# Four graph layers on one core: rows that empty edge slots read, and the order of the last twelve halves of two attentions

## The reference, cut to what matters

```python
x = _layernorm(x + _L0_gnn_ref(...))   # two GCN convolutions
x = _layernorm(x + _L1_gnn_ref(...))   # GAT attention, 8 heads
x = _layernorm(x + _L2_gnn_ref(...))   # HGT attention, 8 heads, 8 node and 8 edge types
x = _layernorm(x + _L3_gnn_ref(...))   # edge pass, summed by src
# the pattern, as in _gat_forward:
e = e_u[src] + e_v[dst]; m = segment_max(e, dst); ex = exp(e - m[dst])
agg = segment_sum(table[src] * (ex / segment_sum(ex, dst)[dst]), dst)
```

## Time and profile before

| | us |
|---|---|
| runs | 7548.39, 7556.19 (median), 7559.97 |
| profiled execution | 7554.35, its span 7552.5 |
| POOL busy | 4883.0 (65% of the span) |
| PE busy, PE weight loads | 4910.9, 3728.8 |
| DVE busy | 4682.7 (62%) |
| ACT busy | 3188.4 (42%) |
| gathers of c1, c2, gat (L757) | x2496, 978 ns each |
| gathers of hgt (L757), edge pass (L2750) | x832 at 982 ns, x832 at 956 ns |

### The profile page before, as it was taken

The page is one execution under the profiler, slowest core; times in us unless marked ns, Lnnn a source line. Parts: engine busy times, 40 slices in busy tenths (PEclk is TensorE's granted clock), DMA queues, the critical chain, the costliest instruction groups (busy, mean ns, idle before and its releaser), DMA issues. The chain is left out here.

```text
span 7552.5 us, 95692 instructions
## 1 busy us (share of the span) xinstructions
PE 4910.9 (65%) x26906; PEld 3728.8 (49%) x26906; DVE 4682.7 (62%) x12437; ACT 3188.4 (42%) x7393; POOL 4883.0 (65%) x4968
## 2 busy tenths in 40 slices
PE   8999801666676777774365655856656666777774
PEld 6777601444444455553254544435555543555553
DVE  8999801555554577775456666645666566566666
ACT  0222200444443444442244444746665642555553
POOL 0677775777776777774777773047777700777774
PEclk9776655888887888886566666967887787899997
DMA  1333201222223222223666665567777822766665
GB/s 29 79 82 79 58 2 28 52 55 55 56 55 48 53 56 55 56 55 56 168 180 183 183 183 118 195 196 230 231 230 224 221 69 82 217 209 210 209 208 146
DMA packets 817681, 925.24 MB, mean 123 GB/s; under 512 B 120147, under 2 KB 656219, under 8 KB 816923
## 3 DMA queue, kind: packets, MB, share of 16 engines
q0 software_dynamic: 198144, 441.54, 23.4%
q1 hardware_dynamic: 395118, 365.43, 16.2%
q10 hardware_dynamic: 223916, 112.15, 5.1%
HBM read 724.85 MB, written 193.87 MB: 122 GB/s over the span
## 5 line engine op out<-in xcount | busy, mean ns | idle before, releaser
L757 POOL DMA_INDIRECT arena<-t,d_src x2496 | 2441.0, 978 | 902.6 <-issue 759.2
L796 PE MATMUL ps<-arena 128*128 128x128 f32 (+2 forms) x8320 | 1779.4, 374 | 755.9 <-DMA arena<-t,d_src 623.5
L796 PEld LDWEIGHTS ps<-arena 128*128 128x128 f32 x8320 | 1567.2, 255 | 1015.7 <-issue 921.6
L805 DVE TENSOR_TENSOR arena<-arena,ps 128x512 f32 (+2 forms) x1040 | 835.4, 803 | 710.4 <-PE ps L796 656.9
L757 POOL DMA_INDIRECT arena<-t,d_typed x832 | 817.2, 982 | 488.8 <-issue 252.7
L721 POOL DMA_INDIRECT d_rec<-arena x784 | 789.0, 1006 | 442.7 <-issue 251.9
L2750 POOL DMA_INDIRECT arena<-t,s_dst x832 | 795.5, 956 | 295.6 <-issue 250.7
L793 PE MATMUL ps<-int_tmp 128*128 128x512 bf16 (+1 forms) x1664 | 554.7, 402 | 475.0 <-DVE arena L805 238.9
L1234 PE MATMUL ps<-arena 128*128 128x416 f16 x3328 | 770.4, 385 | 0.0
L1975 PE MATMUL ps<-arena 128*128 x2496 | 408.5, 296 | 451.7 <-ACT arena L1870 294.2
L1173 ACT ACTIVATE arena<-arena 128x128 f16<-128x128 f16 x1664 | 662.6, 480 | 6.9
(11 more groups left out here) (451 smaller groups left out, 8054.2 us busy)
## 6 DMA issues: line engine op xcount, KB each, us to landing
spill<-arena ACTq DMA_DIRECT2D x208, 512.0 KB, 4.2
arena<-spill SPq DMA_DIRECT2D x208, 512.0 KB, 5.1
arena<-d_loT SPq DMA_DIRECT2D x208, 256.0 KB, 5.0
arena<-s_loT SPq DMA_DIRECT2D x104, 512.0 KB, 4.9
arena<-key_d SPq DMA_DIRECT2D x98, 512.0 KB
t<-arena SPq DMA_DIRECT2D x49, 1024.0 KB, 4.4
arena<-t,d_src POOLq DMA_INDIRECT x2496
arena<-t,d_typed POOLq DMA_INDIRECT x832
```

The source lines that it names most:

```text
L757: pool.indirect_dma_start(out=rows[r][:, i, :], out_offset=None, in_=table, in_offset=bass.IndirectOffsetOnAxis(ap=idx[:, 8 * n + i:8 * n ...
L796: return nc.tensor.matmul(self.banks[i // 4][:, bass.ds(self.slot[i], self.width)], weights, rows, start=False, stop=False, skip_group_che ...
L805: nc.vector.tensor_tensor(at, at, got, ALU.add).then_inc(self.added, 1)
```

## The change

- **Empty slots.** The fill pattern gets SPREAD = 7 times c in the source and `typ` fields, where c is the slot's number modulo 832 (so neighbouring slots are seven rows apart). The 352 pads get 49 times their lane, for which ACT's copies of those two fields are split, behind a new semaphore. On the side sorted by source, empty slots get 49 times the lane, by one small operation and one of 128x832 more in `decoded`.
- **Tails of both attentions.** The last window's scan now comes ahead of the weighing from half 93 on, in new orders of ACT, PE and DVE. `at` has four buffers in the tail (the two new ones lie over `hot_T`, free once the last exponent products are done). Halves 96 to 99 are read back early into four buffers of their own (`m_last`), issued by SP before halves 94 and 95. Halves 100 to 103 are neither sent to DRAM nor read back: their messages are formed from the ring buffers `rows`, and ACT doesn't wait for their landing.

```diff
--- before.py
+++ after.py
...
+SPREAD, LANE_SPREAD = 7, 49
...
+                for f in (0, 2):
+                    nc.scalar.activation(d_recs[:, FULL_ROWS:UC, f], iota_part[:, 0:1].to_broadcast([P, UC - FULL_ROWS]), ACT.Copy, scale=float(LANE_SPREAD)).then_inc(pads_set, 1)
                 for f, n in enumerate(("src", "dst", "typ", "wgt")):
-                    nc.scalar.activation(d_recs[:, :, f], e_in[n], ACT.Copy)
+                    if n in ("src", "typ"):
+                        nc.scalar.activation(d_recs[:, 0:FULL_ROWS, f], e_in[n][:, 0:FULL_ROWS], ACT.Copy)
+                        act.wait_ge(pads_set, 2)
+                        nc.scalar.activation(d_recs[0:TAIL, FULL_ROWS, f:f + 1], e_in[n][0:TAIL, FULL_ROWS:FULL_ROWS + 1], ACT.Copy)
+                    else:
+                        nc.scalar.activation(d_recs[:, :, f], e_in[n], ACT.Copy)
...
-                step(nc.vector.memset(fill, 0.0))
-                nc.vector.memset(fill.rearrange("p (c r) -> p c r", r=4)[:, :, 1], PAD_KEY).then_inc(fill_set, 1)
                 dve.wait_ge(iota_done, 1)
                 step(nc.vector.tensor_copy(iota_c, iota_ci))
+                fields = fill.rearrange("p (c r) -> p c r", r=4)
+                step(nc.vector.memset(fill, 0.0))
+                step(nc.vector.memset(fields[:, :, 1], PAD_KEY))
+                nc.vector.tensor_scalar(fields[:, :, 0:4:2], bcast_last(iota_c, 2), float(SPREAD), None, ALU.mult).then_inc(fill_set, 1)
...
+                    step(nc.vector.tensor_scalar(spread, iota_part[:, 0:1], LANE_SPREAD / (2 * P), None, ALU.mult))
...
+                    step(nc.vector.scalar_tensor_tensor(dec_h, dec_i, spread, dec_h, ALU.mult, ALU.add))
                     step(nc.vector.scalar_tensor_tensor(s_dst[:, 0:SC], dec_a, 0.0, dec_h, ALU.max, ALU.add))
...
-            at = arena[:, 7680:7680 + 2048].rearrange("p (b c n) -> p b c n", b=2, c=8)
+            at = arena[:, 7680:7680 + 4096].rearrange("p (b c n) -> p b c n", b=4, c=8)
...
+            LEFT, AGAIN, KEPT = HALVES - LAG, HALVES - 2 * RING, HALVES - RING
+            o_last = rows_at[-1] + 8 * width if gat else AT_Q
+            m_last = arena[:, o_last:o_last + RING * 8 * W].rearrange("p (b c f) -> p b c f", b=RING, c=8)
...
+            def at_of(n):
+
+                return at[:, n % 2] if n < LEFT else at[:, (n - LEFT) % 4]
+
+            def m_of(n):
+
+                if AGAIN <= n < KEPT:
+                    return m_last[:, n - AGAIN]
+                return m_last[:, n - KEPT - 2] if n >= KEPT + 2 else m[:, n % 2]
+
+            def m_before(n):
+
+                return n - 2 if n < AGAIN else n - 6
...
-                    for k in range(TURNS4 - LAG // RING, TURNS4):
-                        for r in range(RING):
-                            reload(RING * k + r, k, r)
+                    for r in range(2):
+                        reload(LEFT + r, LEFT // RING, r)
+                    if not gat:
+                        sp.wait_ge(exp_ps, 2 * HALVES)
+                    for r in range(RING):
+                        sp.wait_ge(spilled[r], 16 * (AGAIN // RING) + 16)
+                        sp.dma_start(m_last[:, r, :, 0:D], spill[bass.ds(AGAIN + r, 1)].rearrange("o p (c f) -> p (o c) f", f=D)).then_inc(last_in[r], 16)
+                    for r in range(2, RING):
+                        reload(LEFT + r, LEFT // RING, r)
...
-                    def edge_hots(n, b):
-                        need(act, mm, 2 * n - 2)
+                    def edge_hots(n):
+                        if n < LEFT + 2:
+                            need(act, mm, 2 * n - 2)
+                        elif n < AGAIN:
+                            act.wait_ge(exp_ps, 2 * HALVES)
+                        else:
+                            act.wait_ge(mm, 2 * n - 6)
                         for i in range(8):
-                            last = nc.scalar.activation(at[:, b, i], iota_row[:, :], ACT.Abs, bias=lw[:, 8 * n + i, 0:1], scale=-1.0)
+                            last = nc.scalar.activation(at_of(n)[:, i], iota_row[:, :], ACT.Abs, bias=lw[:, 8 * n + i, 0:1], scale=-1.0)
                         last.then_inc(far, 1)
                         act.wait_ge(far, n + 1)
-                        nc.scalar.activation(at[:, b], at[:, b], ACT.Relu, bias=ones[:, 0:1], scale=-1.0).then_inc(hot, 1)
-
-                    def denominators(v, j, b):
+                        nc.scalar.activation(at_of(n), at_of(n), ACT.Relu, bias=ones[:, 0:1], scale=-1.0).then_inc(hot, 1)
+
+                    def denominators(v, j):
+                        n = WH * v + j
                         act.wait_ge(e_ready, v + 1)
-                        nc.scalar.activation(m[:, b, :, D:W].rearrange("p (z c) h -> p z c h", z=2), in_half(v, j), ACT.Copy).then_inc(den, 1)
+                        if LEFT + 2 <= n < AGAIN:
+                            act.wait_ge(mm, 2 * m_before(n) + 2)
+                        nc.scalar.activation(m_of(n)[:, :, D:W].rearrange("p (z c) h -> p z c h", z=2), in_half(v, j), ACT.Copy).then_inc(den, 1)
...
-                        act.wait_ge(landed[j % RING], base + 128 * (WH // RING * w + j // RING) + 128)
-                        act.dma_start(spill[bass.ds(n, 1)].rearrange("o p (c f) -> p (o c) f", f=D),
-                                      rows[j % RING][:, :, keep:keep + D]).then_inc(spilled[j % RING], 16)
+                        if n < KEPT:
+                            act.wait_ge(landed[j % RING], base + 128 * (WH // RING * w + j // RING) + 128)
+                            act.dma_start(spill[bass.ds(n, 1)].rearrange("o p (c f) -> p (o c) f", f=D),
+                                          rows[j % RING][:, :, keep:keep + D]).then_inc(spilled[j % RING], 16)
...
-                    for j in range(LAG):
-                        if j == 4:
-                            exponentials(v)
-                            put_back(v)
-                        edge_hots(HALVES - LAG + j, j % 2)
-                        denominators(*lagging(WINDOWS, j), j % 2)
+                    for j in range(3):
+                        edge_hots(LEFT + j)
+                        denominators(*lagging(WINDOWS, j))
                         if j == 0:
                             raise_scores(v)
                             keep_keys(v)
+                    edge_hots(LEFT + 3)
+                    edge_hots(LEFT + 4)
+                    exponentials(v)
+                    put_back(v)
+                    for j in range(3, LAG):
+                        if j > 4:
+                            edge_hots(LEFT + j)
+                        denominators(*lagging(WINDOWS, j))
...
-                    v, left = WINDOWS - 1, HALVES - LAG
+                    v = WINDOWS - 1
                     raise_window(v)
-                    weigh(left, 0, 0)
+                    weigh(LEFT, 0)
                     row_of(v, 0)
-                    weigh(left, 0, 1)
+                    weigh(LEFT, 1)
                     column_of(v, 0)
-                    weigh(left + 1, 1, 0)
                     row_of(v, 1)
-                    weigh(left + 1, 1, 1)
                     column_of(v, 1)
-                    weigh(left + 2, 0, 0)
+                    weigh(LEFT + 1, 0)
+                    weigh(LEFT + 1, 1)
                     lower_window(v)
-                    weigh(left + 2, 0, 1)
+                    weigh(LEFT + 2, 0)
+                    weigh(LEFT + 2, 1)
...
-                        dve.wait_ge(back_in[b], 16 * k + 16)
+                        if n < AGAIN:
+                            dve.wait_ge(back_in[b], 16 * k + 16)
+                        elif n < KEPT:
+                            dve.wait_ge(last_in[n - AGAIN], 16)
+                        else:
+                            dve.wait_ge(mm, 2 * m_before(n) + 2)
                         dve.wait_ge(e_ready, v + 1)
                         for z in range(2):
                             ex = in_half(v, j)[:, z]
-                            part_m = m[:, b, 4 * z:4 * z + 4, 0:D]
+                            part_m = m_of(n)[:, 4 * z:4 * z + 4, 0:D]
+                            got = part_m if n < KEPT else rows[n % RING][:, 4 * z:4 * z + 4, keep:keep + D]
                             if head_last:
-                                part_m = part_m.rearrange("p c (d h) -> p c d h", h=H)
+                                part_m, got = (a.rearrange("p c (d h) -> p c d h", h=H) for a in (part_m, got))
                                 ex = ex.unsqueeze(2).to_broadcast([P, 4, DK, H])
                             else:
-                                part_m = part_m.rearrange("p c (h d) -> p c h d", h=H)
+                                part_m, got = (a.rearrange("p c (h d) -> p c h d", h=H) for a in (part_m, got))
                                 ex = ex.unsqueeze(3).to_broadcast([P, 4, H, DK])
-                            nc.vector.tensor_tensor(part_m, part_m, ex, ALU.mult).then_inc(msg, 1)
```

(26 more changed lines are left out.)

14 lines of the change are left out of this document (7 added, 7 removed).

## The result

The changed kernel takes 7465.27 us in the median of 4 runs (7461.23 to 7470.68), the kernel before 7556.81 in the same set. The ratio is 0.9883, 95% interval 0.9869 to 0.9898. The profiled execution took 7470.68, its span 7468.9; against the 7554.35 of before that is 83.7 us less. The forecast was 7474, and 7473.5 for the profiled execution.

The account below looks back on a forecast made before the run. POOL's gather stream was taken to bound each pass, with slow landings and attention tails behind it. Landing 57.4, tails 18.6 and 7.5, less 2.7 cost, took 80.8 off 7554.35: 7473.5, said as 7474, range 7457 to 7498 us.

Parts of the forecast that it names:

- The landing: Ends of all five passes: with spread rows, the lag behind POOL's last gather falls to mid pass's, 57.4 us gained.
- the clock's 3 us: Last halves of five passes: a busier PE might keep its higher clock, 3 us more, left to the range.
- The cost: Histogram stage and `decoded`: DVE's added operations for spread rows cost 2.7 us, 2.5 of them for the fill pattern.
- hgt's tail: After hgt's last gather: fewer read-backs and new order cut DVE's waits from 24.5 to 5.9 us, gaining 18.6.
- gat's tail: After gat's last gather: same edits, but node steps keep DVE busy; of 12.4 us of waits, 7.5 gained.
- The sum: Whole kernel: 57.4 + 18.6 + 7.5 - 2.7 = 80.8 us off the profiled 7554.35, giving 7473.5.
- A: Rival at the passes' ends: slow packets come from load or filling queues, not the equal row; 7531 us, 6%.
- B: Rival in the attention tails: DVE's waits pass to ACT, PE or half 95's reload; 7494.7 us, 10%.
- C: Rival in POOL's gathers: spread rows cost POOL time per gather; at 40 ns each, 7640 us, 3%.
- D: Rival in the edge pass: the side sorted by source stays at one row and keeps its lag; 7483 us, 3%.

Follow-up runs that it names:

- spread_again: Kernel before with the spread rows of empty slots alone, old tails, run once more: 7495.85 us, ratio 0.9922 to the kernel before.
- tails_again: Kernel before with the new attention tails alone, empty slots still reading one row, run once more: 7525.03 us, ratio 0.9963 to the kernel before.
- late_reload: Changed kernel with halves 96 to 99 read back behind 94 and 95, waiting for the product of half n-2: 7472.32 us in one run.
- two_at: Changed kernel with two buffers of 0/1 matrices in the tail in place of four: 7483.20 us in one run.
- pe_later: Changed kernel with PE's node-step transposition in gat's tail moved behind the first half of the next weighing: 7485.99 us in one run.
- near_rows: Changed kernel with empty slots reading neighbouring rows, one row on the side sorted by source: 8713.23 us in one run, in a set of 8734 us.
- spread_only: Kernel before with the spread rows alone, first time, in a set where the kernel before took 8733.77 us: 8724.80 us, ratio 0.9986.
- changed_again: Changed kernel as it is, run again in a set where the kernel before took 8741.67 us: ratio 0.9947.

## Why the prediction was right

- *The landing*, 57.4 us forecast. By its own measure the lags fell by 10.1, 9.65, 15.05, 14.85 and 9.7, 59.4 in all; the 2.0 us more come from the attentions, where the middle's lag of 2.70 was taken and 1.62 and 1.89 were reached. The stretches behind c1, c2 and the edge pass fell by 0.8, 0.8 and 1.1 more than the lags. In c1 and c2 that is the size of what PE's eight products gained, 1.15 and 1.26 for 2.07 us: the clock's 3 us that stood in the range only. Step and size right; shown by spread_again (58 us less, cost taken off).
- *The cost*, 2.7 us forecast. The start to the first gather is 3.4 us longer, but 1.8 us stand in the trace of the histogram stage ahead of any DVE instruction that was changed. The new operation took 1.03 us, not 2.05. L433, which priced it at 1.02 for 832 elements a partition, reads PSUM; the new one reads and writes SBUF, as does L431, which took 0.65 for 832. From the cast of the weights that ends ahead of the edit to the counts it is 6.8 us for 5.6, so +1.1. The term was oversized by 1.6 us, as far as one trace tells: the first gather of tails_again, which lacks this edit, comes at 1322.8, that of before at 1325.5.
- *hgt's tail*, 18.6 forecast. From DVE's first message behind the scoring (6066.2) to the last sum (6140.5) it took 74.3 us, after 54.7 (6013.0 to 6067.7), so 19.6. What stays, one wait of 3.0 for half 95 and scan rows of 0.7 each, is nearly what was written, and by late_reload and two_at each of the two edits carries its part.
- *gat's tail*, 7.5 forecast. It gave 4.4 against the trace of before (79.3 to 74.9 us), and 6.6 between before and tails_again. The step that failed is that of DVE's 12.4 us of waits only 4.9 stay, and with it that the waits for PE go: they are 5.1 for 5.2. With the read-back (2.2), ACT (1.3) and a scan row (0.5), 9.1 us stay. PE's waits at the node steps and its clock behind them are what the trace shows in its place; pe_later did not prove them the cause.
- *The sum*: 80.8 forecast, 83.7 measured in the profiled executions. The errors are +2.0 and +2.7 (lags, and the stretches behind them), +1.0 (hgt), -3.1 (gat), -0.7 (start) and +0.6 in the POOL streams, 2.5 in all; the last 0.4 lies between the two ways of measuring. That the sum comes within 3 us is partly luck: gat's shortfall is covered by lag and clock.
- *The rivals.* A falls: the slow packets came from the equal row; with 54 GB/s at c1's end instead of 39 they take 249 ns instead of 1550, so it isn't load. The Trainium skill's "HBM Reference", section Latency, names load as what makes an access slow; here the same row did, at less traffic, and the measurement decides. B falls by tails_again (29 us; hgt's measure 19.4 less), though two_at shows how near ACT is. C falls: the median is 947 ns before and after. D's price is right in kind where the side is left out (near_rows), but the change doesn't leave it out.
- *A reading that was off.* The prediction speaks of 128 packets of the same row. In c1 they are 128 rows in 16 packets of eight; no number of the sum hangs on it.
- *What the prediction didn't see*: that its largest term needs consumers that are ahead. It said so of this kernel's pace (6.4 to 7.2 us of every 10) and was right; where PE pauses by itself, POOL starts a gather every 1.45 us, less lag builds, and what goes of it gives a fraction (spread_only, 0.9986).

## What to carry to other kernels

Padding entries of an index list should read different rows; two by turns were enough here, where a gather is issued every 1.25 us and two rows take 0.83. To price such a fix, compare two rates, that at which gathers are issued and that at which the equal row is served; only the difference, times the number of gathers that read one row alone, stands as a lag at the end of each pass. It is worth its full length only where the issuing engine is fast and the engines that use the rows wait for them. In a tail that drains a pipeline, count for each wait which engine's buffers set it: here two more matrix buffers were worth 9 us and an early read-back 6, both behind a wait that named another engine.

## What the hardware showed that was not expected

- One row of a table was served about every 13 ns (a gather of 128 rows every 1.63 to 1.86 us over the last 16 gathers of each pass), nearly whatever the row's size: 1.69, 1.63 and 1.77 us for 512, 512 and 544 bytes, 1.86 for 1024, 1.68 for 1536. It is a rate of reads, not of bytes.
- A gather that reads two rows by turns lay 0.83 us between its first packet's start and its last one's end, one of a single row 1.4 to 1.7 even with nothing queued, one of many rows 0.53. So each row has its own rate of about 13 ns a read, and two of them are served side by side.
- In two sets the same program took 15.6% longer, with PE pausing between products for nothing that the profile shows, and the gain of this change shrank from 1.17% to 0.53% with it. The cause is open. It isn't shown to be the chip: the record numbers the chips, and number 3 stands beside a set of 7554 us (spread_again) and one of 8742 (changed_again).
